# A causal attention's maximum pass: the triangle added by VectorE within the maximum, and narrow chunks that share a bank

## The reference

```python
attn = jnp.einsum('bhqd,bhkd->bhqk', q, k) / math.sqrt(HEAD_DIM)
attn = attn + alibi_bias(seq_len, N_HEADS)[None] + causal_mask(seq_len)[None, None]
attn = jax.nn.softmax(attn, axis=-1)
y = jnp.einsum('bhqk,bhkd->bhqd', attn, v)
```

## Time and profile before

| | |
|---|---|
| median of 3 runs | 2741.91 us (2739.04 to 2743.98) |
| the profiled execution's own time | 2740.84 us |
| its span, first to last instruction | 2739.0 us |
| TensorE (PE) busy | 2578.6 us, 94% |
| VectorE (DVE) busy | 1841.4 us, 67% |
| ScalarE (ACT) busy | 1269.8 us, 46% |
| GpSimd (POOL) busy | 788.9 us, 29% |
| mean granted TensorE clock | 0.973 |

### The profile page before, as it was taken

How to read it: one execution, slowest core, us unless ns; L and a number is a source line. 1 busy time by engine, 2 the same in 40 slices (tenths; PEclk the granted TensorE clock), 3 DMA queues, 4 the chain that set the end, 5 groups by cost and what they waited for, 6 DMA issues and landing times. The chain is left out here.

```text
span 2739.0 us, 38708 instructions
## 1 busy us (share of the span) xinstructions
PE 2578.6 (94%) x14106; PEld 1256.2 (46%) x14106; DVE 1841.4 (67%) x3926; ACT 1269.8 (46%) x1936; POOL 788.9 (29%) x760
## 2 busy tenths in 40 slices
PE   5987999999999999898999998999999999899998
PEld 3543333333333332454555664444544554555665
DVE  6858888788787885584664336787677675565334
ACT  4441666566566667543222222465455557321321
POOL 2545214123141300155424532211122100333441
PEclk8997999999999999999999999999999999999999
DMA  4003330330303400003213655534322340311665
GB/s 127 1 18 92 65 53 24 54 63 14 58 25 53 65 1 2 1 1 101 65 50 94 150 110 130 101 60 59 64 53 44 65 59 2 115 35 35 141 156 162
DMA packets 162592, 175.76 MB, mean 64 GB/s; under 512 B 19090, under 2 KB 135762, under 8 KB 162258
## 3 DMA queue, kind: packets, MB, share of 16 engines
q1 hardware_dynamic: 146948, 152.57, 25.4%
q0 software_dynamic: 12416, 17.84, 3.8%
q10 hardware_dynamic: 3040, 2.88, 0.4%
HBM read 116.32 MB, written 56.13 MB: 63 GB/s over the span
## 5 line engine op out<-in xcount | busy, mean ns | idle before, releaser
L1856 DVE TENSOR_REDUCE a_mx<-a_bank 128x1 f32<-128x512 f32 (+3 forms) x1792 | 1035.5, 628 | 240.3 <-PE a_bank L1589 171.9
L1724 ACT ACTIVATE a_E<-a_bank 128x1024 f32<-128x1024 f32 (+3 forms) x896 | 796.4, 931 | 400.9 <-PE a_bank L1647 272.9
L1589 PE MATMUL a_bank<-a_KT,a_QT 96*128 96x512 bf16 (+4 forms) x1792 | 572.8, 368 | 26.0 <-DVE a_mx L1856 16.1
L1647 PE MATMUL a_bank<-a_QT,a_KT 99*128 99x512 bf16 (+4 forms) x1792 | 504.6, 356 | 4.0 <-DMA a_QT<-a_mT 1.9
L1662 PE MATMUL a_bank<-a_E,a_Vg 128*32 128x512 f32 (+3 forms) x3584 | 436.5, 559 | 0.7 <-ACT a_E L1724 0.7
L1589 PEld LDWEIGHTS a_bank<-a_KT,a_QT 96*128 96x128 bf16 (+1 forms) x1792 | 152.3, 98 | 491.8 <-DVE a_mx L1856 310.1
L1647 PEld LDWEIGHTS a_bank<-a_QT,a_KT 99*128 99x128 bf16 (+1 forms) x1792 | 169.5, 98 | 172.5 <-ACT a_E L1724 31.4
L436 POOL TENSOR_TENSOR f_hl<-f_hT,f_hh 128x512 f16<-128x512 f32 x96 | 110.8, 1157 | 333.3 <-ACT f_hh L453 333.0
L897 PE MATMUL d_bank<-wdT,d_hT 128*128 128x256 f32 (+1 forms) x768 | 193.6, 395 | 4.2 <-DVE d_hT L1094 4.2
L1008 ACT ACTIVATE d_silu<-d_bank 128x512 f32<-128x512 f32 x96 | 57.1, 595 | 269.7 <-PE d_bank L882 269.6
L897 PEld LDWEIGHTS d_bank<-wdT,d_hT 128*128 128x128 f32 (+1 forms) x768 | 140.9, 192 | 63.6 <-issue 43.6
(11 more groups left out here) (234 smaller groups left out, 3592.2 us busy)
## 6 DMA issues: line engine op xcount, KB each, us to landing
parts<-a_parts SPq DMA_DIRECT2D x64, 384.0 KB, 2.6
a_QT<-parts SPq DMA_DIRECT2D x180, 128.0 KB, 5.6
a_KT<-parts SPq DMA_DIRECT2D x180, 128.0 KB, 8.7
d_wgu<-in_L_ffn_w_gate SPq DMA_DIRECT2D x64, 176.0 KB
d_wgu<-in_L_ffn_w_up SPq DMA_DIRECT2D x64, 176.0 KB
d_wd<-in_L_ffn_w_down SPq DMA_DIRECT2D x64, 176.0 KB
normalised<-d_xn SPq DMA_DIRECT2D x8, 1152.0 KB, 4.7
acc<-d_zero SPq DMA_DIRECT2D x2, 4224.0 KB, 16.0
```

Of the source, the lines that this page charges most:

```text
L1589: last = nc.tensor.matmul(out[:, 0:w], QT[0:W, h, qt * P:(qt + 1) * P], KT[0:W, h, kh * HALF:kh * HALF + w], start=True, stop=not diag)
L1647: last = nc.tensor.matmul(out, KT[:, h, kt * P:(kt + 1) * P], QT[:, h, half * HALF + c0:(half + 1) * HALF], start=True, stop=not diag)
L1724: nc.scalar.activation(E[:, u % 2, 2 * pair:2 * pair + 2, c0:HALF], bank[:, 2 * pair:2 * pair + 2, c0:HALF], ACT.Exp).then_inc(exps, 1)
L1856: nc.vector.tensor_reduce(mx[:, x[1] // C % 2, j, qt, kh:kh + 1], out[:, 0:w], AX.X, ALU.max).then_inc(freed_dve, 1)
```

## The change

Five things, all for `second`. A diagonal chunk has no triangle matmul any more; VectorE adds the triangle in the pass that takes the maximum (`tensor_tensor_reduce`: add `causal`, maximum, the sum written back to the bank), and a second instruction reads the maximum out. `causal` is 512 wide, zero but for the triangle in its last 128 columns, so its right end of width `w` fits every diagonal chunk. Narrow chunks share a bank: 128 with 384 of one head, 256 with 256 of two heads. A group so fills 36 banks for 48, with the same 48 chunks; in the second half of queries the whole chunks and the others are dealt out evenly. `AHEAD` becomes 15 banks (still five units), a unit gets three banks, and `between` has smaller numbers. The triangle of the score pass stays on TensorE, with `causal` as the weights and `ident_b` as the moving side. `masks` and the constant `mask_kq` go, and `bnr` now lies in the room of `yT`.

```diff
+    def piece(j, qt, kh, at_=0):
+
+        return j, qt, kh, min(HALF, (qt + 1) * P - kh * HALF) if second else HALF, at_
+
+    chunks = []
+    if second:
+        for h in range(QH):
+            for j in range(0, GH, 2):
+                q = h * KPH
+                whole = [[piece(i, qt, 0)] for i in (j, j + 1) for qt in range(q, q + KPH)] if h else []
+                edge = [[piece(i, q, h), piece(i, q + 2, h, P)] for i in (j, j + 1)]
+                edge += [[piece(j, q + 1, h), piece(j + 1, q + 1, h, 2 * P)]] + [[piece(i, q + 3, h)] for i in (j, j + 1)]
+                step = (len(whole) + len(edge)) / len(edge)
+                for n in range(len(whole) + len(edge)):
+                    chunks.append(edge.pop(0) if not whole or edge and n >= (5 - len(edge)) * step else whole.pop(0))
...
-        between[(16 + 4 * k) if second else (44 + 4 * k)] = ("tokens", 1, k)
-        between[(31 + 4 * k) if second else (62 + 4 * k)] = ("value", 1, k)
+        between[(12 + 3 * k) if second else (44 + 4 * k)] = ("tokens", 1, k)
+        between[(24 + 3 * k) if second else (62 + 4 * k)] = ("value", 1, k)
...
-        between[(33 + 4 * n) if second else (59 + 8 * n)] = ("proj", 1, n)
+        between[(25 + 3 * n) if second else (59 + 8 * n)] = ("proj", 1, n)
...
-            masks = sb(tag + "masks", [P, 2, P], BF16)
-            bnr = sb(tag + "bnr", [P, NT - TPB, 6])
+            causal = sb(tag + "causal", [P, HALF], BF16)
+            bnr = yT.rearrange("p a k c -> p (a k c)")[:, 0:(NT - TPB) * 6].rearrange("p (t s) -> p t s", s=6)
...
-                        diag = second and qt * P < kh * HALF + w <= (qt + 1) * P
-                        last = nc.tensor.matmul(out[:, 0:w], QT[0:W, h, qt * P:(qt + 1) * P], KT[0:W, h, kh * HALF:kh * HALF + w],
-                                                start=True, stop=not diag)
-                        if diag:
-                            last = nc.tensor.matmul(out[:, w - P:w], ident_b[:], masks[:, 0, :], start=False, stop=True)
+                        for j, qt, kh, w, at_ in pieces:
+                            h = G % NG * GH + j
+                            last = nc.tensor.matmul(out[:, at_:at_ + w], QT[0:W, h, qt * P:(qt + 1) * P], KT[0:W, h, kh * HALF:kh * HALF + w],
+                                                    start=True, stop=True)
...
-                            last = nc.tensor.matmul(out[:, 0:P], ident_b[:], masks[:, 1, :], start=False, stop=True)
+                            last = nc.tensor.matmul(out[:, 0:P], causal[:, HALF - P:HALF], ident_b[:], start=False, stop=True)
...
-                        j, qt, kh, w = chunks[x[1] % C]
-                        nc.vector.tensor_reduce(mx[:, x[1] // C % 2, j, qt, kh:kh + 1], out[:, 0:w], AX.X, ALU.max).then_inc(freed_dve, 1)
+                        for j, qt, kh, w, at_ in chunks[x[1] % C]:
+                            dst, src = mx[:, x[1] // C % 2, j, qt, kh:kh + 1], out[:, at_:at_ + w]
+                            if second and qt * P < kh * HALF + w <= (qt + 1) * P:
+                                last = nc.vector.tensor_tensor_reduce(out=src, in0=src, in1=causal[:, HALF - w:HALF], scale=1.0,
+                                                                      scalar=LOWEST, op0=ALU.add, op1=ALU.max, accum_out=dst)
+                            else:
+                                last = nc.vector.tensor_reduce(dst, src, AX.X, ALU.max)
+                        last.then_inc(freed_dve, 1)
...
-                    nc.vector.tensor_copy(masks[:, 0, :], core.const("mask_qk"))
-                    nc.vector.tensor_copy(masks[:, 1, :], core.const("mask_kq")).then_inc(masked, 1)
+                    nc.vector.memset(causal[:, 0:HALF - P], 0.0).then_inc(masked, 1)
+                    nc.vector.tensor_copy(causal[:, HALF - P:HALF], core.const("mask_qk")).then_inc(masked, 1)
+                    dve.wait_ge(masked, START + 2)
```

18 lines of the change are left out of this document (9 added, 9 removed).

## The result

The changed kernel takes 2707.82 us (median of 4 runs, 2707.04 to 2709.49) beside 2742.23 us of the kernel before (4 runs, 2739.04 to 2743.98). The ratio is 0.9873, with a 95% interval of 0.9860 to 0.9885: 34.4 us less. The direction was forecast, the size was not.

The account below looks back on a forecast made before the run. TensorE was taken to set the pace, VectorE second. First and last groups -4, middle groups -15.9, opening +1.5 gave -18.4 us, from 2740.84 to 2722.4; against the runs' median, forecast 2723 us, range 2710 to 2756.

Parts of the forecast that it names:

- Removed from TensorE: Maximum pass of the second attention: 512 triangle matmuls go, 58 ns each; the steady 464 worth 26.9 us at most.
- the fifth rival: Maximum pass: it keeps its triangles on TensorE, so the change does not do what it says; no chance given.
- Added to VectorE: 512 of 768 maxima become a pass plus a read; surplus taken as 100 ns a pair, range 70 to 260.
- I let the waits grow by 2.5 us: Middle 400 us of the steady part: sharing and dealing out banks lengthen waits, cutting 18.4 us to 15.9.
- First and last groups: 1750 to 1850 and 2250 to 2300 us: with VectorE at 95%, 150 us become 146, gain 4.
- Middle groups: Middle 400 us of the steady part: TensorE falls by 18.4 us, VectorE reaches 83% of it; gain 15.9.
- Opening: 1700 to 1750 us: pairs add 2.2 us until 1720, triangles then save 0.8; together a loss of 1.5.
- Preparation: A memset and one cast replace two casts of 2.4 us, ahead of VectorE's 7.79 us idle: nothing either way.
- The first one: Steady part: VectorE absorbs 70 ns pairs, whole 26.9 us gained less 1 for the opening; 2716 us, chance 0.18.
- The second: Diagonal chunks: the read waits until the pass has left VectorE, 162 ns a pair; 2738 us, chance 0.13.
- the third: Chunks waiting for a bank: slow reads, 250 ns a pair, make VectorE the bound; 2758 us, chance 0.17.
- The fourth: Diagonal passes reading and writing the same bank take two cycles per number, 0.43 us more with the read; 2845 us, chance 0.10.

Follow-up runs that it names:

- Clumping: The changed kernel with two of a unit's three fills together behind the product; projections, transposes and outputs there move behind it too: 2730.25 us, ratio 0.9964.
- three operations more: The changed kernel with three more one-number memsets on VectorE behind each diagonal pass (1536 in all): 2720.41 us, ratio 0.9927.

## Why the prediction was wrong

**What bounds the kernel**: right. TensorE sets the pace, VectorE is second, and the one place where TensorE's next step is late is a chunk that waits for its bank. The prediction named that place and then didn't follow what the change does to it.

**Removed from TensorE**: right, as a count and as a price. 512 matmuls are gone, and 58 ns each stand for 26.9 us in the steady part. It fell by 31.7, which leaves 4.8 for waits. The scores' own triangle stayed, so the fifth rival fell.

**Added to VectorE, the failed term "I take 100 ns"**. It measured 49 ns in a row of pairs and 32 to 37 ns in the steady part, below even the low end of 70. The argument added a small operation (70 ns a step) to a pass that steps like a maximum. A read of one number doesn't take a step of its own: the next pass starts within 20 ns of it. What a pair does cost is seen only as the difference of the starts. With the surplus raised to some 90 ns the ratio was 0.9927, and the forecast had been 0.9931.

**The sharing, the failed step "I let the waits grow by 2.5 us"**. The waits shrank: by about 5 us in groups 3 to 12, which gained 23.4 with 18.4 of triangles. By itself the sharing is worth 17.0 us, with no instruction less on either engine. The sentence before it had the reason in it, "the ring of three spans a whole unit", and set it off against two passes a bank and the dealing, by feeling. The dealing is worth nothing that shows, and the two passes follow each other without a wait. Why 36 banks help can be said in this kernel's terms. With four fills a unit on three banks, the fourth takes the bank that the first one filled in the same unit, two of the four stand together behind the product, and their bank is late. With three fills, each comes back to its bank one whole unit later, at the same place of it (where a unit holds chunks alone; projections and transposes take turns in the same ring). Clumping, with all that it moves, costs 22 us, and a ring of two 54. That spreading four fills gained nothing is measured too. I read it as the distance, still shorter than a unit, being the tighter of the two bounds, but no run separates these, and it stays argued.

**First and last groups, the failed step "with VectorE at 95% the stretch takes 146 us. Gain 4"**. These groups gained 8.3, as much as their triangles are worth (147 x 58 ns = 8.5). In the first 100 us TensorE was busy for 100.00 us with VectorE at 88.7, not at 98%. The 95% was a rule of thumb with no row behind it, fed with a pair's price twice too high. It fails at its own price too: with three operations more, a pair some 80 to 90 ns dearer than a maximum, the same groups still gained 6.7.

**Middle groups, "gain 15.9"**: it was 23.4, by the price of the pair and the sharing. VectorE was expected at 83% there and shows 79%. That the forecast comes near what a pair of 90 ns would give is luck, by two errors of opposite sign. It counted 19.9 us for the steady part and all of it for the triangle's removal, though with 48 banks that gives 11.2 there (584.2 to 573.0), and 17.6 with no cost on VectorE at all (to 566.6). And it credited the sharing, which lets the rest through, with less than nothing.

**Opening, "+1.5"**: the first score starts 1.8 us earlier for 1.5 later. The pairs do cost there (VectorE is busy for all of 8.00 us from 1742 to 1750, and has 17.44 of the first 20), but a group has fewer fills. I don't build on it: the first maximum itself starts between 1701.6 and 1707.0 us in the fourteen profiles, and at 1704.0 and 1704.1 in these two.

**Preparation**: right. As the timeline of VectorE has it, a memset of 0.22 us and one cast of 2.19 lie ahead of an idle time of 7.98 us on VectorE.

**The rivals.** The first one was nearest: cover holds, TensorE gets it all, "down to 2710 if some of the old 8.1 us of idle goes too". That idle went to 1.6 us, and 26.9 + 6.5 = 33.4 is close to the 31.7 of the steady part; what kept it above the result was 1 us for the opening, where 1.8 came in. Its sign, a TensorE wait that halves, was only partly there (92.6 to 72.1 us). Most of that wait lies under matmuls in the array: TensorE's idle time before chunks is 1.6 us beside it. It got 0.18, for an argument ("against it: the first and last groups") that rested on the price of the pair. The second needed 162 ns and the third 250: false. The fourth, a slow pass that writes its own bank, is false too: 704 ns shown for 512 numbers against 687 for a maximum, and steps of 0.65 and 0.61 us.

The Trainium skill, "VectorE: DVE Perf Modes", stood against a low price with "The DRAIN you can't avoid". I had read that section too narrowly: it adds that a next operation that is not held starts earlier, and the section "Two Vector instructions with no wait between them" counts the accumulator's read as an instruction of its own, held if it starts in another group of 32 partitions than the last output did. (Its other ground, a scalar read through a pointer by the instruction in front, is not given here: the pass has a constant.) All of these start at partition 0, so by that rule nothing is held. The trace agrees: read and next pass start together at 1710.56 and 1711.21 us. The Trainium skill, "Vector Engine (DVE) Microarchitecture Reference", section 7, gives half the rate to one family of instructions with two SBUF sources that are not bf16; it doesn't name this pass as one of them. Here one source is in a bank and the other is bf16, and 704 ns beside 687 shows no halving.

## What to carry to other kernels

When a ring of buffers feeds one engine from another, count the fills in one repetition of the order against the ring's size before costing instructions: with as many fills as banks, each at a place of its own, this kernel gained 17 us without one instruction less, and with one fill more in a third of the units it lost 15 to 19 of 34 us. An edit that frees the bounding engine pays only as far as the ring lets it through, so two edits that look independent are to be costed together (11.9 and 17.0 us apart, 34.4 together). And take the price of a small operation from the distance between the starts of its neighbours, not from its shown length.

## What was not expected of the hardware

- A pass with a running maximum plus the read of it is shown with 704 + 140 ns and steps by 0.62 to 0.65 us, where a plain maximum of the same width steps by 0.61. The read and the next pass start together or 20 ns apart.
- A memset of one number, shown with 59 ns, moves the next pass by some 10 ns if it is alone behind the read. Three of them move it by 40 to 50 ns in the opening and by 70 in the steady rows shown (0.69 for 0.62 us). Such an operation is a poor dose for an experiment unless its step is read first.
- Writing the sum back to the bank that is being read costs next to nothing beside a maximum that writes one number (704 against 687 ns shown for 512 numbers).
- A bias of one number per partition makes an exponential over 1024 numbers longer, 904 ns shown for 816 (means over nearly the same mix of widths).
